# Down products of batches two to four from half-precision operands, with a bound worked out from the rounded weights

## The reference, cut to what matters

```python
x = L0_attn_x                                    # (4, 512, 512) float32: four batches
x = x + attn(layernorm(x), W_q, W_kv, W_o)       # per-head FFT, normalize, cumsum along the sequence, ifft, W_o
x = x + ffn(layernorm(x), gate_w, up_w, down_w, gate_scale, up_scale, down_scale)

def ffn(x, ...):                                 # H = 512, I = 1536
    gate = silu(qmm(x, gate_w, gate_scale))
    up   = qmm(x, up_w, up_scale)
    return qmm(gate * up, down_w, down_scale)

def qmm(x, w, scale):
    wq = w.astype(float8_e4m3fn).astype(x.dtype) # the weight is rounded to 8 bits, the rest stays float32
    return (x @ wq) * scale
```

## Time and profile before

| | |
|---|---|
| median of 3 runs | 422.8 us (421.98 to 423.19) |
| the profiled execution, own time | 422.29 us |
| its span | 420.4 us |
| granted TensorE clock, mean | 0.998 |
| PE busy | 411.4 us, 98% of the span |
| DVE busy | 281.6 us, 67% |
| ACT busy | 193.2 us, 46% |
| POOL busy | 102.7 us, 24% |
| HBM read / written | 17.44 MB / 4.19 MB |

### The profile page before, as it was taken

How to read it: one execution, slowest core, us unless ns; L and a number is a source line. 1 busy time by engine, 2 the same in 40 slices (tenths; PEclk the granted TensorE clock), 3 DMA queues, 4 the chain that set the end, 5 groups by cost and what they waited for, 6 DMA issues and landing times.

```text
span 420.4 us, 5467 instructions
## 1 busy us (share of the span) xinstructions
PE 411.4 (98%) x1895; PEld 218.9 (52%) x1895; DVE 281.6 (67%) x497; ACT 193.2 (46%) x322; POOL 102.7 (24%) x108
## 2 busy tenths in 40 slices
PE   8999999999999999999999999999999999999994
PEld 4744444455555554554554564454555555555553
DVE  5999998999999695187685953176774744322234
ACT  3687656576746245436322573255342522132220
POOL 0133641014244222045450031043441001300003
PEclk9999999999999999999999999999999999999999
DMA  8996648700271133241112025320112051200002
GB/s 259 272 244 238 176 101 163 164 2 0 62 241 26 30 73 77 49 150 49 27 27 50 2 50 89 63 80 22 25 28 51 0 89 32 80 2 0 2 0 100
DMA packets 57546, 33.54 MB, mean 80 GB/s; under 512 B 49456, under 2 KB 49840, under 8 KB 57392
## 3 DMA queue, kind: packets, MB, share of 16 engines
q1 hardware_dynamic: 57088, 32.93, 31.1%
q10 hardware_dynamic: 432, 0.28, 0.2%
HBM read 17.44 MB, written 4.19 MB: 51 GB/s over the span
## 4 chain that ended last, share of the span: by engine, by line
PE 82%; DMA 4%; DVE 4%; SPq 3%; ACT 3%; POOL 1%; issue 1%; POOLq 0%; DVEq 0%
PE bd L449 20%; PE bg L433 20%; PE bu L433 20%; PE ba L350 10%; PE ba L390 7%; SPq L1606 2%; PE bd L350 2%; PE ba L363 1%; DMA h<-x_dram 1%; DMA hT<-w_q_dram 1%; DMA xT<-xs 1%; POOL xs L1495 1%; PE bd L336 1%; ACT half L708 1%; DMA hT<-ks 1%
## 5 line engine op out<-in xcount | busy, mean ns | idle before, releaser
L449 PE MATMUL bd<-dw,fu 128*128 128x512 f32 x376 | 100.0, 411 | 0.0
L433 PE MATMUL bg<-hT,gu 128*128 128x512 f16 x384 | 91.0, 380 | 0.9 <-DMA hT<-ks 0.9
L433 PE MATMUL bu<-hT,gu 128*128 128x512 f16 x384 | 90.7, 379 | 0.0
L449 PEld LDWEIGHTS bd<-dw,fu 128*128 128x128 f32 x376 | 70.6, 188 | 18.6 <-DVE fu L1152 0.7
L1147 DVE SCALAR_TENSOR_TENSOR ff<-bu,us,sl 128x512 f32<-128x512 f32 x48 | 35.9, 748 | 65.6 <-PE bu L433 62.4
L695 ACT ACTIVATE sl<-bg,gs 128x512 f32<-128x512 f32 x48 | 33.0, 687 | 80.5 <-PE bg L433 79.6
L350 PE MATMUL ba<-wf,xT 128*128 128x512 f16 x288 | 63.2, 379 | 0.0
L433 PEld LDWEIGHTS bu<-hT,gu 128*128 128x128 f16 x384 | 37.6, 98 | 45.3
L433 PEld LDWEIGHTS bg<-hT,gu 128*128 128x128 f16 x384 | 34.9, 98 | 47.5 <-issue 9.8
L1152 DVE TENSOR_TENSOR fu<-ff,fu 128x512 fp32r<-128x512 f32 x47 | 40.1, 854 | 15.7 <-ACT fu L701 15.3
L1521 POOL TENSOR_TENSOR h<-ff,h 128x512 f32<-128x512 f32 x14 | 17.6, 1276 | 129.8 <-DVE ff L1173 129.8
(11 more groups left out here) (178 smaller groups left out, 447.9 us busy)
## 6 DMA issues: line engine op xcount, KB each, us to landing
h<-x_dram SPq DMA_DIRECT2D x16, 256.0 KB, 4.2
out_dram<-h SPq DMA_DIRECT2D x15, 256.0 KB, 2.0
hT<-w_q_dram SPq DMA_DIRECT2D x4, 256.0 KB, 4.2
gu<-w_kv_dram SPq DMA_DIRECT2D x4, 256.0 KB, 4.0
hT<-gate_w_dram SPq DMA_DIRECT2D x2, 512.0 KB, 3.7
hT<-up_w_dram SPq DMA_DIRECT2D x2, 512.0 KB, 6.0
gu<-woT_dram SPq DMA_DIRECT2D x1, 1024.0 KB, 5.5
hT<-down_w_dram SPq DMA_DIRECT2D x2, 512.0 KB, 4.8
```

The costliest lines, as they stand in the source:

```text
L433: m = e.matmul(bk[:, :], gu[:, c, 4 * w + k, col:col + P], hT[:, b % 2, part, k, :], start=k == 0 and part == 0, stop=k == KT - 1 and part ...
L449: m = e.matmul(bd[t][:, :], fu_at(n)[:, part, P * t:P * t + P], dw[:, i, :], start=i == 0 and part == 0, stop=i == NI - 1 and part == 1)
```

## The change

- The down products of batches 1 to 3 use half-precision operands: ACT copies `dw` into `dw16` (twelve copies, 128x512 each), which lies over `own`, and `fu` of these batches lives in the four places of `zT` (half precision) in place of the two of `fu`; `pT` as a 33rd place goes.
- So that the products fit the range of half precision, they are divided by a bound: `us2 = us / bound`, `ds2 = ds * bound`. The bound is worked out on the chip: twelve reductions on DVE over the rounded gate and up weights (`dve_peak_of`, one for each piece, 128x1024 to 128x4), a few small ones (`dve_peak`), a pair of matmuls with the identity (`pe_peak`), `dve_peak_all` (a reduction on one partition and two instructions on a single element), a matmul with a row of ones (`pe_bound`), and `dve_bound`.
- Since `own` is now wanted for `dw16`, the last pieces 15 to 17 are staged in `n1` (over `hT` of batch 1), and so wait for the rounding of pieces 13 to 15.
- The orders of all five lists are new, in batch 0 and in the loop. Before the gate products of batch 0 there are now three more `dve_round`; `pe_down(12 b - 1)` stands behind the first query product of the next batch and ahead of `pe_gate_up(b, 0)`.

```diff
 STAGE = (("n0", 0), ("n0", 1), ("x2", 0), ("x2", 1), ("g1", 0), ("g1", 1), ("g2", 0), ("g2", 1), ("e", 0),
-         ("e", 1), ("e", 2), ("n1", 0), ("n1", 1), ("n1", 0), ("n1", 1), ("e", 0), ("e", 1), ("e", 2))
+         ("e", 1), ("e", 2), ("n1", 0), ("n1", 1), ("n1", 0), ("n1", 1), ("n1", 0), ("n1", 1), ("n1", 0))
...
+        dw16 = own[:, :, :].rearrange("p s n -> p (s n)").bitcast(F16).rearrange("p (i n) -> p i n", n=512)
...
         def fu_at(n):
-            return pT[:, :, :] if n == NB * NI - 1 else fu[:, n % 2, :, :]
+            return fu[:, n % 2, :, :] if n < NI else zT[:, n % 4, :, :]
...
+        def pe_peak(e):
+            vacant(e, ("bound", 0))
+            e.wait_ge(v_top, NI + 3)
+            e.wait_ge(d_id, 16)
+            for n in range(2):
+                m = e.matmul(ba[AT["bound", 0]][0:1, P * n:P * n + P], top[:, n:n + 1], ident, start=True, stop=True)
+            m.then_inc(s_bound, 1)
+
+        def pe_bound(e):
+            vacant(e, ("bound", 1))
+            e.wait_ge(v_peak, 4)
+            e.matmul(ba[AT["bound", 1]][:, 0:1], ones[0:1, :], top[0:1, 3:4], start=True, stop=True).then_inc(s_bound, 1)
...
+            if b == 1 and t == 0:
+                e.wait_ge(a_dw, i + 1)
             for part in range(2):
-                m = e.matmul(bd[t][:, :], fu_at(n)[:, part, P * t:P * t + P], dw[:, i, :],
+                m = e.matmul(bd[t][:, :], fu_at(n)[:, part, P * t:P * t + P], (dw if b == 0 else dw16)[:, i, :],
...
             pe_down(e, 9)
+            pe_peak(e)
             pe_down(e, 10)
+            pe_bound(e)
...
             for b in range(1, NB):
                 nxt = b + 1
                 if nxt < NB:
                     pe_qk(e, nxt, 0, 0)
+                pe_down(e, b * NI - 1)
...
                 pe_gate_up(e, b, 0)
-                pe_down(e, b * NI - 1)
...
+        def act_dw(e, i):
+            e.wait_ge(*rounded(max(10, 3 * (i // 2) + 2)))
+            e.activation(dw16[:, i, :], dw[:, i, :].bitcast(F32), ACT.Copy).then_inc(a_dw, 1)
...
+        def dve_peak_of(e, n):
+            first = 16 + 4 * (2 * (n // 3) + n % 3)
+            e.wait_ge(*rounded(n))
+            e.tensor_reduce(top[:, first:first + 4], pairs[n][1], AX.X, ALU.max, apply_absolute_value=True).then_inc(v_top, 1)
+
+        def dve_peak(e):
+            e.wait_ge(d_sc, 48)
+            e.tensor_tensor(top[:, 4:16], gs[:, :], us[:, :], ALU.mult).then_inc(v_top, 1)
+            e.wait_ge(v_top, NI + 1)
+            e.tensor_reduce(top[:, 0:1], top[:, 16:64], AX.X, ALU.max).then_inc(v_top, 1)
+            e.tensor_reduce(top[:, 1:2], top[:, 4:16], AX.X, ALU.max, apply_absolute_value=True).then_inc(v_top, 1)
+
+        def dve_peak_all(e):
+            e.wait_ge(s_bound, 1)
+            both = ba[AT["bound", 0]][0:1, 0:256].rearrange("p (a n) -> p a n", a=2)
+            e.tensor_reduce(top[0:1, 2:4], both, AX.X, ALU.max).then_inc(v_peak, 2)
...
+
+        def dve_bound(e):
+            e.wait_ge(s_bound, 2)
+            e.tensor_scalar(top[:, 0:1], ba[AT["bound", 1]][:, 0:1], 1.0 * D * D / 2.0 ** 15, None, ALU.mult).then_inc(v_bound, 2)
+            e.wait_ge(v_bound, 2)
+            e.reciprocal(top[:, 1:2], top[:, 0:1]).then_inc(v_bound, 1)
+            e.wait_ge(v_bound, 3)
+            e.tensor_scalar(us2[:, :], us[:, :], top[:, 1:2], None, ALU.mult).then_inc(v_bound, 1)
+            e.tensor_scalar(ds2[:, :], ds[:, :], top[:, 0:1], None, ALU.mult).then_inc(v_bound, 1)
```

More of the change, by code:

```diff
@@ L169, in build @@
         v_half = sem("dve_half")
+        s_bound, a_dw, v_top, v_peak, v_bound = (
+            sem(n) for n in ("pe_bound", "act_dw", "dve_top", "dve_peak", "dve_bound"))
         v_f, v_fu, v_y, v_out, v_near, v_rd = (
@@ L1305, in vector_program @@
-            dve_scale(e, 1, 0, 0)
-            dve_fu(e, 1)
-            dve_round(e, 7)
-            dve_f(e, 2)
-            dve_product(e, 1, 0)
-            dve_round(e, 8)
+            dve_round(e, 10)
+            dve_stats1(e, 2, 1)
+            dve_scale(e, 1, 0, 0)
+            dve_f(e, 2)
+            dve_scale(e, 1, 1, 1)
+            dve_product(e, 1, 0)
+            dve_fu(e, 1)
+            dve_stats1(e, 2, 2)
+            dve_fu(e, 2)
+            dve_scale(e, 1, 2, 1)
+            dve_peak_of(e, 1)
@@ L1311, in vector_program @@
             dve_f(e, 3)
-            dve_stats1(e, 2, 3)
-            dve_fu(e, 2)
+            dve_peak_of(e, 3)
+            dve_round(e, 11)
+            dve_scale(e, 1, 3, 1)
             dve_fu(e, 3)
-            dve_root0_head(e, 2, range(NT))
-            dve_round(e, 9)
-            dve_root0_tail(e, 2, range(NT))
-            dve_round(e, 10)
             dve_f(e, 4)
             dve_scale(e, 1, 1, 0)
+            dve_stats1(e, 2, 3)
             dve_product(e, 1, 1)
+            dve_f(e, 5)
@@ L1322, in vector_program @@
+            dve_root0_head(e, 2, range(NT))
+            dve_round(e, 12)
+            dve_fu(e, 4)
+            dve_f(e, 6)
+            dve_peak_of(e, 4)
+            dve_peak_of(e, 6)
             dve_zl(e, 1, 0)
+            dve_peak_of(e, 7)
+            dve_fu(e, 5)
             dve_scale(e, 1, 2, 0)
+            dve_round(e, 13)
+            dve_zl(e, 1, 1)
+            dve_root0_tail(e, 2, range(NT))
+            dve_fu(e, 6)
+            dve_f(e, 7)
+            dve_round(e, 14)
+            dve_product(e, 1, 2)
@@ L1324, in vector_program @@
+            dve_round(e, 15)
+            dve_peak_of(e, 9)
+            dve_f(e, 8)
+            dve_peak_of(e, 10)
+            dve_fu(e, 7)
+            dve_scale(e, 1, 3, 0)
+            dve_fu(e, 8)
+            dve_round(e, 16)
             dve_xn(e, 2, 0)
-            dve_f(e, 5)
-            dve_round(e, 11)
-            dve_fu(e, 4)
+            dve_peak_of(e, 12)
             dve_xn(e, 2, 1)
-            dve_round(e, 12)
-            dve_f(e, 6)
-            dve_scale(e, 1, 3, 1)
-            dve_fu(e, 5)
@@ L1359, in vector_program @@
+            dve_peak(e)
+            dve_xn(e, 2, 3)
+            dve_fu(e, 10)
+            dve_o(e, 1, 2)
+            dve_o(e, 1, 3)
+            dve_peak_all(e)
+            dve_f(e, 11)
             dve_ln2_head(e, 1, range(NT))
+            dve_bound(e)
+            dve_fu(e, 11)
             dve_ln2_tail(e, 1, range(NT))
@@ L1373, in vector_program @@
                 nxt = b + 1
+                dve_scale_out(e, b - 1, 0)
                 if nxt < NB:
@@ L1430, in vector_program @@
                     dve_product(e, nxt, 3)
-                    dve_zl(e, nxt, 2)
+                dve_f(e, b * NI + 7)
+                if b + 2 < NB:
+                    dve_root0_tail(e, b + 2, range(NT))
+                dve_fu(e, b * NI + 6)
+                if nxt < NB:
+                    dve_o(e, nxt, 1)
                     dve_zl(e, nxt, 3)
-                    dve_o(e, nxt, 1)
                     dve_o(e, nxt, 2)
-                dve_f(e, b * NI + 7)
+                dve_f(e, b * NI + 8)
                 if nxt < NB:
```

569 lines of the change are left out of this document (296 added, 273 removed).

## The result

The changed kernel takes 428.2 us (median of 4 runs, 426.3 to 429.9) against 423.0 for the kernel before on the same chip: ratio 1.0131, interval 1.0105 to 1.0157. It is slower, as forecast, but by 5.2 us and not by 2.4. The profiled execution took 428.74 us, with a span of 426.9 (420.4 before).

A forecast was written before the change was run, and what follows sets the result against it. PE was taken as the bound, with VectorE beside it for the first 160 us. 422.29 - 4.2 + 6.6 = 424.7, and 0.5 more for the median gives 425.2 against 422.8; range 419.5 to 429.

The forecast's parts named there:

- net wait of 6.6 us: Ahead of batch 1's first gate product: late VectorE delays hT queue, PE's start 8.45 us later, less 1.84 for pe_down 11.
- The matmuls, 4.2 us: Down products on PE: 288 matmuls change to half precision, each 14.5 ns shorter, gaining 4.2 us.
- rival 4: Down products: the 15 ns come from switching accumulation groups, so no gain and 429.4 us; chance 0.05.
- VectorE's cost, 16.0 us: Before batch 1's transposes: twelve reductions at 1.14 us make 13.7, with the small instructions 16.0 us added.
- Rival 1: VectorE in batch 0's feed-forward: reductions take 0.6 us each, 9.5 us added, no net wait worth naming, 418.7 us; chance 0.17.
- Nothing is taken from DVE: VectorE's cost before batch 1's transposes: the change only adds work there and removes none.
- What hides it: VectorE's 11.4 us free time up to batch 1's last dve_hT hides 7.7 of 16.0 us, leaving 8.3 us late.
- Rival 2: VectorE's free time takes all it can, 11.4 us; net wait 2.9, total 421.5 us; chance 0.18.
- As DVE is full on both sides, this only says where PE waits.: Around batch 0's first gated product: moving three roundings ahead and three dve_stats1 behind was given no cost of its own.
- The small ones: pe_peak and pe_bound: under 0.6 us, inside PE's wait; dve_scale_out's later place in the loop: 0 to 0.5, taken as 0.
- one of my signs of a wrong forecast: The forecast is wrong if batch 1's first gate product starts before 179 us or PE waits again in batches 2 to 4.
- rival 3: VectorE passes lengthen beside other work and PE's waits add up: 10.5 us unhidden, net wait 8.8, 428.4 us; chance 0.10.

The follow-up runs named there:

- the fastest version: Kernel before's lists with half-precision products, reductions spread among batch 2's query sums, ScalarE's sixth-group query copies ahead of batch 1's first silu: 419.9 us, ratio 0.9932.
- short reductions: Changed kernel with the twelve reductions reading only 8 values of each run of 256: 427.3 us, ratio 1.0127.
- the moved call: Changed kernel with act_half(3) on ScalarE put back behind the last low part of the output weights: 425.5 us, ratio 1.0081.
- the run with copies spread: Kernel before with half precision in batches 3 and 4 only, ScalarE's twelve down-weight copies placed two or four at a time in its gaps: 423.2 us, ratio 1.0026.
- both edits: Changed kernel with act_half(3) put back behind the output weights' low parts and the reductions reading 8 of each 256 values: 425.8 us, ratio 1.0081.

## Why the prediction was wrong

The direction was right and the reason wrong. The step that failed is the net wait of 6.6 us for VectorE ahead of batch 1's gate product: it was 0. In its place stood a step that I had put at nothing, the new order ahead of batch 0's first gate product: 8.27 us. Step by step:

**The matmuls, 4.2 us.** Right. The block of the earlier trace rows went from 5.30 to 5.18 us (344.84 to 350.02), which also settles rival 4. From batch 1's first gate product on, the changed kernel gains 3.2; it waits 0.22, 0.42 and 0.21 us there, where the kernel before shows no wait. In the fastest version the stretch from that product is 418.6 - 175.07 = 243.5 against 246.4, 2.9 less; the two products of the bound take 0.53 + 0.31 us of PE from start to start, with 0.2 of gaps beside them, and two waits 0.45: about 4.4 in all.

**VectorE's cost, 16.0 us.** Right for what was added: 1206 ns a reduction, 1.14 from start to start, and 2.3 us for the small ones. Rival 1 (0.6 us) is out. But "Nothing is taken from DVE" was not right: up to its last `dve_hT` of batch 1 VectorE was busy 154.75 us, against 144.33 before, 10.4 more. Passes that both kernels have were shorter in the new lists: the eighteen clamps of the weight pieces averaged 0.69 us instead of 0.82, the twelve `dve_fu` 0.70 instead of 0.81, the twelve `dve_xn` 0.54 instead of 0.65. The last section shows beside what the long ones stood. The rule of the Trainium skill (VectorE: DVE Perf Modes, The perf-mode tier table), no faster mode for tensor_reduce on 16-bit data, agrees with these 1.21 us for 1024 values.

**What hides it; from DVE to PE, net wait 6.6 us.** This step failed. SP's queue started even later than I had it (171.13, I had 167.9), yet PE was not waiting when `hT` landed: PE itself was 8.27 us later by then, and its own work had grown by 1.84 + 0.53 + 0.31. Counted from batch 0's first gate product the queue started 80.90 us behind, where it was 77.03 before (158.99 - 81.96): 3.9 later and not 8.9, and as late with short reductions. I had 7.7 of the 16.0 us hidden; in these lists all of the load was. Three things made room: VectorE's gaps, the shorter passes, and three roundings that now stand ahead of that product. There was little to spare: the last transpose was issued near 182.8, such a transpose takes 2.5 us (median) to land here, and PE came at 185.50 (an estimate of 0.2 us). The same 95.27 us without the load, and the same ratio with and without it beside the moved call, show that the net wait was 0. My sum took batch 1's gate product as bound by VectorE and let PE arrive on time. The load does cost, 9.2 us, in lists that were not laid out for it; there it shows as many waits and not as the one that I priced. Rival 2, that the free time takes all and the lists are rearranged, was nearest for this step.

**"As DVE is full on both sides, this only says where PE waits."** This sentence was the wrong one. It dismissed the rearrangement ahead of the first gated product, on all five queues, as free. It cost 8.27 us in the profiled execution: waits of 1.73, 3.03 and 2.76, where the earlier trace rows has 0.88 for the last, and 1.7 of lowered clock account for most. The 8.27 is of one execution: with short reductions, which change little ahead of that product, it stood at 87.24. I had counted the instructions added, and had not followed the moved ones against the landing of what they need, though the new list has `act_half(3)` ahead of `act_qk(0, 3, 1)` on ScalarE. That move is shown by experiment (about 2 us). That the rest comes from the lists and not from the load is shown too: with half precision and bound on the old lists, the first gate product stands at 81.7 to 83.0, and at 81.84 in the version that has the full load and the same one reduction ahead of it. Which other moves carry it was not taken apart.

**The sum.** 420.4 + 8.27 + 3.23 - 5.0 = 426.9. My terms, -4.2 and +6.6, gave +2.4 by one true figure and one that was absent, in the place of a larger one that I had set to nothing. That the direction came out right is luck.

**The small ones.** `pe_peak` and `pe_bound` were to be under 0.6 us and hidden; they are not hidden where PE has no wait, 0.84 from start to start. In batches 2 to 4 PE waits the 0.85 us above, where I took 0 out of 0 to 0.5. The order there can be charged with the 0.42 at most: the waits of 0.22 and 0.21 for POOL stand in the versions on the old lists too. PE waiting again there was one of my signs of a wrong forecast. Two readings were slightly off, without weight: a third of the small gaps is 1.95 us and not 2.1, and SP's issues lie 0.09 and 0.11 us apart and not 0.05. PE has no wait where ScalarE's copies stand in the changed kernel, as forecast, but the run with copies spread shows that this depends on which gaps they take.

## What to carry to other kernels

When a change comes with rearranged instruction lists, walk each in-order engine's moved entries against the time at which their inputs land: here one entry moved ahead of critical work cost about 2 us, and 12 us of added work, in lists that had room for it, nothing that could be measured. A gap can take work only if nothing on the path waits for the instruction behind it. And before a delay is charged to the main engine, ask when that engine itself would arrive: two late engines do not add.

## What the runs showed of the hardware that I had not expected

After a wait of PE, what follows may run at the lower clock: 0.55 granted for 3.4 us behind a wait of 3.03, and behind a wait of 9.34 a clock of 0.50 over the first 3.1 us, with 4.74 us in place of 2.75 for 12 matmuls. The length of the wait alone does not decide it. At one and the same place, ahead of batch 0's first gate product, the changed kernel waited 2.76 us and its 8 matmuls took 1.89 at a granted clock of 1.00, while with both edits the wait was 2.11 and they took 3.55 at 0.50:
```profile
86.05 3.55 PE L444 MATMUL bg<-hT,gu 128*128 128x512 f16 x8 [2.11 <-DMA hT<-ks]
```
What else decides it stays open here.

Some VectorE passes are much longer beside an instruction of POOL. In the kernel before, a weight clamp that ran wholly beside POOL's work took 1.64 us, where the fifteen with POOL idle averaged 0.68, and a normalization took 1.38 where nine averaged 0.54:
```profile
115.85 1.64 DVE L991 TENSOR_SCALAR near<-hT 128x1024 fp8e4<-128x1024 f32 x1
115.61 1.33 POOL L1495 TENSOR_TENSOR xs<-xn,xs 128x512 f16<-128x512 f32 x1
```
The long reductions of the bound took 1.21 us either way in the changed kernel (four wholly beside POOL's work, two with POOL idle), and the gated products `dve_f` 0.75 either way in the kernel before. This answers what rival 3 had noticed, the same clamp at 676 and 928 ns. The rows show that the two go together in time, and not by what they hinder each other.
